# A Fourier layer tower on one core: three two-bank slots for the skip products, two banks for the transforms, and a new order of TensorE's work

## The reference

```python
v = concat([x, gx, gy]) @ p_w + p_b            # 3 features a pixel -> 32 channels
for i in range(4):
    x_ft = rfft2(v)
    out1 = einsum('bixy,ioxy->boxy', x_ft[:, :, :12, :12], W1)
    out2 = einsum('bixy,ioxy->boxy', x_ft[:, :, -12:, :12], W2)
    x1 = irfft2(out_ft)                        # out_ft: out1, out2, zero elsewhere
    x2 = einsum('bcxy,cd->bdxy', v, w_w[i]) + w_b[i]
    v = batch_norm(x1 + x2)
    if i < 3: v = relu(v)
h = einsum('bcxy,cu->bxyu', v, q_w) + q_b
```

## Time and profile before

| | us |
|---|---|
| median of 3 runs | 1845.2 |
| lowest and highest of them | 1844.68, 1857.29 |
| the profiled execution | 1830.84 |
| its span, first to last instruction | 1828.6 |
| PE, DVE, ACT, POOL busy | 1420.0, 686.7, 638.9, 289.6 |

### The profile page before, as it was taken

The page is one execution under the profiler, slowest core; times in us unless marked ns, Lnnn a source line. Parts: engine busy times, 40 slices in busy tenths (PEclk is TensorE's granted clock), DMA queues, the critical chain, the costliest instruction groups (busy, mean ns, idle before and its releaser), DMA issues.

```text
span 1828.6 us, 39520 instructions
## 1 busy us (share of the span) xinstructions
PE 1420.0 (78%) x18015; PEld 820.4 (45%) x18015; DVE 686.7 (38%) x678; ACT 638.9 (35%) x918; POOL 289.6 (16%) x405
## 2 busy tenths in 40 slices
PE   3567589999957779899875777888988488807887
PEld 3434266656533335555443333445545363207831
DVE  6432244554522224453442222444443231067443
ACT  1232145555522215555542221445545231000230
POOL 4630302021032200202204230020202231100000
PEclk8777699999977769999987776988989798955676
DMA  3668677777227869999943776999997316820001
GB/s 96 155 168 232 197 174 181 196 186 180 77 73 212 237 185 264 299 321 304 277 94 89 214 236 187 255 233 298 265 289 199 121 51 234 342 56 1 1 0 23
DMA packets 189377, 329.17 MB, mean 180 GB/s; under 512 B 27507, under 2 KB 133379, under 8 KB 170515
## 3 DMA queue, kind: packets, MB, share of 16 engines
q1 hardware_dynamic: 173644, 289.69, 57.4%
q0 software_dynamic: 15568, 36.98, 8.4%
HBM read 165.09 MB, written 142.64 MB: 168 GB/s over the span
## 4 chain that ended last, share of the span: by engine, by line
PE 60%; ACT 11%; DMA 11%; DVE 9%; issue 4%; SPq 3%; POOL 1%; DVEq 0%; ACTq 0%
PE ps L1332 10%; PE ps L1369 9%; PE ps L1294 6%; PE ps L1271 6%; DMA arena<-half_inverse 5%; PE ps L1389 5%; ACT ps L1172 4%; PE ps L1358 4%; PE ps L1280 3%; PE ps L1401 3%; ACT arena L1163 2%; PE ps L1447 2%; ACT arena L821 2%; PE ps L536 2%; DVE arena L821 2%
## 5 line engine op out<-in xcount | busy, mean ns | idle before, releaser
L1675 DVE STREAM_TRANSPOSE arena<-ps 128x1024 f32<-128x1024 f32 x96 | 179.1, 1950 | 422.7 <-PE ps L1389 422.7
L1036 POOL DMA_DIRECT2D arena<-arena x192 | 110.6, 584 | 891.8 <-ACT arena L1180 889.4
L1369 PE MATMUL ps<-arena 48*128 48x128 f32 x3072 | 212.2, 290 | 41.1 <-DMA arena<-half_inverse 30.2
L1369 PEld LDWEIGHTS ps<-arena 48*128 48x128 f32 x3072 | 191.9, 198 | 110.2 <-issue 69.9
L1163 ACT ACTIVATE arena<-ps,arena 128x1024 f32<-128x1024 f32 x128 | 147.4, 1202 | 262.5 <-PE ps L1369 256.9
L1172 ACT ACTIVATE ps<-ps 128x1024 f32<-128x1024 f32 x192 | 194.0, 1011 | 56.7 <-PE ps L1332 56.4
L1271 PE MATMUL ps<-arena 64*64 64x64 f32 x2304 | 144.8, 285 | 62.2 <-DMA arena<-arena 62.2
L1332 PE MATMUL ps<-arena 32*32 32x512 f32 x2944 | 187.9, 635 | 5.1 <-issue 4.6
L1271 PEld LDWEIGHTS ps<-arena 64*64 64x64 f32 x2304 | 136.3, 166 | 121.7 <-issue 121.7
L1665 DVE STREAM_TRANSPOSE arena<-arena 128x2048 f32<-128x2048 f32 x64 | 146.3, 2300 | 65.7 <-ACT arena L1163 41.0
L1389 PE MATMUL ps<-arena 32*32 32x512 f32 x3072 | 156.9, 606 | 5.7 <-DVE arena L1665 3.0
(11 more groups left out here) (286 smaller groups left out, 1317.7 us busy)
## 6 DMA issues: line engine op xcount, KB each, us to landing
maps<-arena SPq DMA_DIRECT2D x56, 1024.0 KB, 7.1
arena<-half_inverse SPq DMA_DIRECT2D x96, 384.0 KB, 11.1
half_inverse<-arena SPq DMA_DIRECT2D x33, 1024.0 KB, 6.1
maps<-inputs SPq DMA_DIRECT2D x28, 1024.0 KB, 11.6
arena<-maps SPq DMA_DIRECT2D x112, 256.0 KB, 9.0
inputs<-maps SPq DMA_DIRECT2D x112, 256.0 KB, 10.0
arena<-in_mode_w POOLq DMA_DIRECT2D x48, 384.0 KB, 3.9
arena<-maps SPq DMA_DIRECT2D x8, 2048.0 KB, 15.2
```

Of the source, the lines that this page charges most:

```text
L1369: last = nc.tensor.matmul(ps[:, b, at:at + 128], gtile[s][rows, 4 * b + 2 * h + n, :], iy[rows, :], start=False, stop=(i >= 2 and n == 1))
L1675: nc.vector.transpose(dst, src).then_inc(y_turned, 1)
```

## The change

1. Banks 0 to 3 in one set become three slots of two banks (0 and 1, 2 and 3, 4 and 5). A unit is now half of a half: `("out", q, h, p)` or `("next", q, h, p)`, where p names its rows of PE: 0 to 63 or 64 to 127. The eight units of a quad go round the three slots in the order of the table `UNITS`. A unit takes a slot once ACT is done with the unit three places earlier.
2. The y transform, the x transform and their results have only banks 6 and 7. The y transform is done in two parts e (rows 0 to 63, rows 64 to 127), and DVE must have turned part 0 before part 1 starts.
3. The inverse products of a unit (`inverse_part`) all read the same rows 64p to 64p+47 and are four in a row for each bank, so `turn_done` goes. For this the layouts of the modes and of `half_inverse` columns change (images b and b+32 in place of neighbours); the number and size of their DMAs stay.
4. The features of the first pass are fp32, 28 images and 3 grid rows in each group of 32 rows, in three blocks, loaded once near the start in 24 DMAs behind a memset of 128x3072 by POOL; no splitting by ACT and DVE. A skip product of the first pass is one fp32 product with 32 rows per bank.
5. The first pass stores a half of a map in four DMAs with rows of 2 KB, so that the second pass loads a half in one DMA with rows of 8 KB. The third pass loads as before. The two `group_load` calls near the end issue four DMAs each in place of two.
6. PE and ACT have a new order.

```diff
+        SLOTS_A = 3
+        def slot_of(l, kind, q, h, p):
+            n = PER_PASS * l + UNITS[kind, q, h, p]
+            return n % SLOTS_A, n // SLOTS_A + 1
...
-            def blocks32(w, source, h, pair, last_one):
+            def blocks32(w, source, h, p, s, last_one):
                 for x in range(4):
-                    for r in (2 * pair, 2 * pair + 1):
-                        rows = slice(32 * r, 32 * r + 32)
+                    for i in range(2):
+                        rows = slice(64 * p + 32 * i, 64 * p + 32 * i + 32)
...
-                            for g in range(4):
-                                at = 1024 * g + 512 * h
-                                nc.tensor.matmul(ps[:, g, :], w[:, 128 * (q % 8):128 * (q % 8) + 128],
-                                                 feats[q // 8][:, at:at + 512], start=(i == 0), stop=False)
+                    for i in range(2):
+                        rows = slice(64 * p + 32 * i, 64 * p + 32 * i + 32)
+                        nc.tensor.matmul(ps[:, 2 * s + i, :], expconv[rows, at:at + 128],
+                                         feats[QUAD * q // FEATURED][rows, 512 * h:512 * h + 512], start=True, stop=False)
...
+            def inverse_part(l, q, h, p, i):
+                s, n = slot_of(l, "out", q, h, p)
+                pe.wait_ge(g_in[q % 2], 32 * (slot_use(l, q) + 1))
+                rows = slice(64 * p, 64 * p + 4 * KY)
+                for k in range(4):
+                    last = nc.tensor.matmul(ps[:, 2 * s + i, 128 * k:128 * k + 128],
+                                            gtile[q % 2][rows, 8 * i + 4 * h + k, :], iy[rows, :], start=False,
+                                            stop=(k == 3))
+                if i:
+                    last.then_inc(a_full[s], 1)
...
+            def y_transform(l, q, e, yh):
+                if yh == 0:
+                    if e:
+                        pe.wait_ge(y_turned, 2 * n + 1)
+                    elif n:
+                        pe.wait_ge(xs_ev, 2 * n)
...
-                        for pair in range(2):
-                            sp.wait_ge(a_free[pair], set_of(l, "out", i, h) + 1)
-                        sp.dma_start(maps_d[l, ORDER[l][i], :, 2048 * h:2048 * h + 2048], half(h_out(l, i), h))\
-                          .then_inc(map_st[i % 2], 16)
+                        map_store(l, i, h)
                         if l:
                             input_load(l, i + 2, h)
```

More of the change, by code:

```diff
@@ L815, in staged, with per_map, stores, loads @@
             return (1 if batch % 2 == 0 else 0) + 2 * l + batch // 2
-        TURNS = (((0, 0), (1, 1)), ((0, 2), (1, 3)), ((0, 1), (1, 0)), ((0, 3), (1, 2)))
+        def per_map(l):
+            return 128 if l == 0 else 32
+        def stores(l, n):
+            return sum(MOVED * per_map(i) for i in range(l)) + n * per_map(l)
+        def loads(l, n):
+            return 16 * n if l == 1 else 16 * MOVED + 64 * n
         def inverse_evac(copy, ky, g):
-            return copy(xhalf[ky % 2].rearrange("p (g b h o) -> p g h b o", g=2, h=2, o=16)[:, g],
-                        ps[:, 6:8, :].rearrange("p h (o b) -> p h b o", o=16))
+            dst = xhalf[ky % 2].rearrange("p (q j s h o) -> p j h q s o", j=2, s=2, h=2, o=16)[:, g]
+            src = ps[:, 6:8, :].rearrange("p h (o q s) -> p h q s o", o=16, s=2)
+            return copy(dst, src)
+        BANKS = (0, 2, 1, 3)
         block = ctx.enter_context(nc.Block())
@@ L953, in _ @@
             for s in range(2):
-                sp.wait_ge(map_st[s], 32 * MOVED * PASSES)
-            for pair in range(2):
-                sp.wait_ge(a_full[pair], PER_PASS * PASSES)
+                sp.wait_ge(map_st[s], stores(PASSES, 0))
+            for s in range(SLOTS_A):
+                sp.wait_ge(a_full[s], slot_count(PASSES, s))
             stream_load(2)
@@ L1373, in next_set @@
-            def next_set(l, q, h):
-                for pair in range(2):
-                    free_pair(l, "next", q, h, pair)
-                    blocks32(wbd[l + 1], h_out(l, q), h, pair, True).then_inc(a_full[pair], 1)
-            def y_transform(l, q, yh):
+                        last = nc.tensor.matmul(ps[32 * x:32 * x + 32, 2 * s + i, :],
+                                                w[rows, 64 * p + 32 * i:64 * p + 32 * i + 32], source[rows, at:at + 512],
+                                                start=True, stop=last_one)
@@ new lines, in blocks32, with skip @@
+                return last
+            def skip(l, q, h, p):
+                s = take_slot(l, "out", q, h, p)
+                if l == 0:
+                    pe.wait_ge(conv_exp, 1)
+                    pe.wait_ge(f_in[QUAD * q // FEATURED], 16 * 8)
+                    for i in range(2):
+                        rows = slice(64 * p + 32 * i, 64 * p + 32 * i + 32)
+                        at = 128 * (q % (FEATURED // QUAD))
+                        nc.tensor.matmul(ps[:, 2 * s + i, :], expconv[rows, at:at + 128],
+                                         feats[QUAD * q // FEATURED][rows, 512 * h:512 * h + 512], start=True, stop=False)
+                elif q >= KEPT:
+                    pe.wait_ge(ld[q % 2][h], loads(l, q // 2))
+                    blocks32(wbd[l], h_in(l, q), h, p, s, False)
+                else:
+                    for i in range(2):
+                        at = 2048 * h + 512 * (2 * p + i)
+                        nc.tensor.matmul(ps[:, 2 * s + i, :], wbd[l], h_in(l, q)[:, at:at + 512], start=True, stop=False)
@@ L1502, in _ @@
             tt(exp3, exp3, prow.unsqueeze(1).broadcast_to([128, BATCH, CHANNELS]), ALU.add).then_inc(exp_ready, 1)
-            for row in (32, 96):
+            for row in range(FEATURED, 128, 32):
                 last = nc.vector.tensor_copy(prt[0:32, row:row + FEATURE_ROWS], pcol[0:32, 1:4])
@@ L1658, in turn_map @@
                 n = quad_of(l, q)
-                for pair in range(2):
-                    dve.wait_ge(a_free[pair], set_of(l, "out", q, h) + 1)
+                wait_free(dve, l, "out", q, h)
                 if n:
-                    dve.wait_ge(y_full, n)
+                    dve.wait_ge(y_full, 2 * n)
                 src = half(h_out(l, q), h).rearrange("p (b u y) -> p b u y", u=2, y=32)
@@ L1694, in _ @@
             dve.wait_ge(q_read, 2)
-            ts(placed[:, 60:64], image_of[:, 0:4], f1, None, ALU.mult).then_inc(z_ready, 1)
+            for j in range(2):
+                last = ts(placed[:, 30 + 32 * j:32 + 32 * j], image_of[:, 2 * j:2 * j + 2], f1, None, ALU.mult)
+            last.then_inc(z_ready, 1)
             dve.wait_ge(pm_ev, 2)
```

324 lines of the change are left out of this document (159 added, 165 removed).

## The result

The changed kernel takes 2145.3 us (median of four runs, 2123.3 to 2163.8) against 1844.9 us of the kernel before on the same chip: a ratio of 1.157, 95% interval 1.147 to 1.167. It is slower, as forecast, but by 300 us where 52 were forecast, and outside the range. (Now and then an execution of any of these kernels comes out one or two per cent longer at a lower granted clock; such runs are counted in the medians of this text but left out of its ratios, and every ratio is to the runs of the kernel before that were made beside it.) The profiled execution took 2152.4 us.

A forecast was written before the change was run, and what follows sets the result against it. PE was taken to bound the first pass, DMA engines or nearly the later two. Terms 37 + 2 + 12.5 + 3 - 3.5 + 1 = +52 on 1830.84 gave 1883 us (1897 as median), range 1868 to 1930.

The forecast's parts named there:

- The parts, first pass, one quad: PE's pieces in a first-pass quad, priced one by one: 19.45 us against 17.13, +37 us in 16 quads.
- three signs of being wrong: First-pass quad under 17 us, L1396 running beside L1420, or PE waiting for ACT L1204 or L1197 over 1 us a quad.
- the two terms named for it: Range terms: waits for the three slots, 0 to 1 us a quad, and the third pass, 0 to +12 us.
- the third pass at 0: Third pass, DMA engines full for 260 us: +3 us taken, 0 if all of PE's work is hidden.
- What the forecast took from the earlier trace: On PE, a change of shape lets the array run empty first, whichever rows are used; 0.84 us of wait seen.
- rival 1: On PE, shapes do not matter on disjoint rows, so units overlap: faster, -66 us, 1779 us; chance 0.15.
- Rival 2: On PE, the drain holds but units overlap better within a shape: first-pass quad 18.05, total 1860 us; chance 0.14.
- The y part's wait: y part 1 waits for DVE's turn of part 0: nothing mid-pass, about 1.9 us at a pass's end, +2 each pass.
- Rival 3: Two banks of y and x become the loop, next y waiting for ACT's copies: +48, 1945 us; chance 0.10.
- the term of -3.5: Feature casts go, one being on the chain with 3.49 us: -3.5 us, between -7 and 0.

The follow-up runs named there:

- rows64: Kernel after with 64 rows in place of 48 in each inverse product of the map passes, the added 16 times zero; 1951.0 us, 1.064 of before.
- probe2: Kernel before plus unread fp32 blocks holding the kernel after's quad pieces; in its order 491 us (clock 0.67), with 48x128 products in turn 269 us (1.00).
- feat: Kernel before with only the change's fp32 features in four groups of 32 rows; 1817.1 us, 0.976 of before.
- pair: Kernel after with both units' inverse products in turn on the two array halves and PE's pieces regrouped; 1798.1 us, 0.973 of before.
- pair64: The kernel pair with 64 rows in place of 48 in each inverse product, 16 of them times zero; 1785.5 us, 0.975 of before.
- probe: Kernel before plus unread fp32 product blocks of several shapes behind its last product; only 48x128 on one half ran at clock 0.50, for 123 us.
- probe3: Kernel before plus unread fp32 blocks varying rows and columns; one-half 48x128 ran at clock 0.50 (0.212 us per instruction), 64x128 at 1.00 (0.111).
- serial: Kernel before with all inverse products of one array half ahead of those of the other; 1944.9 us, one run.

## Why the prediction was wrong

**The step that failed** is the price list under "The parts, first pass, one quad". Every price there was read at a granted clock of 1.00 (in a pass at 0.98 by the earlier trace rows), and the sum took for granted that a PE with more to do and less to wait for would keep that clock. It did not: 0.71, 0.81 and 0.75 in the three passes. The forecast never named the clock of after as an unknown, so neither the range nor a rival held it, and of its three signs of being wrong (a quad under 17 us, L1396 beside L1420, waits for ACT) none came true. With the clock given back (rows64), 199 of the 322 us are gone. The lower end of the forecast's range, 1868, also lies below what the two terms named for it allow (the third pass at 0 gives 1894), which makes no difference here.

The Trainium skill, "TensorE: Matmul & The Clock Gate", section "What's actually happening", has the clock set "based on how busy the PE has been recently". The trace does not bear that out in the sense of the profile's busy share: 0.74 at 150.00 of 150 us busy here, 1.00 at 145.37 before.

**The rest, point by point.** rows64 shows what the change costs at full clock. One quad of its first pass:

```profile
404.73 1.07 PE ps L1380 x8
405.80 1.98 PE ps L1396 x16
407.78 1.06 PE ps L1380 x4
...
409.85 1.09 PE ps L1396 x8
410.94 1.02 PE ps L1420 x16
411.95 1.09 PE ps L1396 x8
...
414.10 2.53 PE ps L1396 x24
...
424.38 1.07 PE ps L1380 x8
```

- The quad: 19.65 us (424.38 - 404.73) against 19.45. The inverse is 1.98 + 1.09 + 1.09 + 2.53 + 1.09 = 7.8 against 7.7, the features 3.2 against 2.9. At full clock the sum of the price list was right to 1%, and its largest item, the inverse, too; the features were 0.3 too low.
- What the forecast took from the earlier trace rows held: the inverse at 411.95, on rows 0 to 63, starts only when the y part before it, on rows 64 to 127 (410.94), is through, and the 16 and 8 instructions cost what one half alone costs. So rival 1 is out.
- The second pass's best quads are 18.7 us in rows64 against 18.6. Rival 2, with 18.05 in the first, is out too.
- The sum, however, is not 1883: rows64's profiled execution is 1953.9. The first pass is 62 us longer than before, where 39 were forecast: its first two quads are at 0.50 until 284 us and take 27 and 33 us, some 21 more than two at full clock. Before, the clock rose at 237 us. The second pass is 35 longer (12.5 forecast) and the third 34 (3 forecast); there too the first two quads take long, 53 and 48 us together. That a new pass starts at 1.2 GHz, and that the new order leaves it later, is the same omission once more. Why 64 rows do not help in those two quads is open; no run was made for it. That they are entered at 0.50 may be part of it, since keeping the clock and bringing it up were not the same in probe2.
- The y part's wait costs nothing in the middle and comes back at the end of a pass, as forecast. In the chain of the kernel after, at the end of the first pass, DVE's turn L1712 stands twice, with y between:

```profile
646.91 1.91 DVE arena L1712
...
648.95 1.09 PE ps L1420 x16
...
651.26 1.90 DVE arena L1712
```

- Rival 3 did not happen: no wait of PE in the passes is put down to ACT's copies L1204, and ACT is no busier (638.5 us for 638.9).
- The feature cast of the earlier trace rows did not hold PE up, so the term of -3.5 was misread. The chain shows ACT's cast from 109.70 on, but PE's first inverse product along x started at 112.97, before that cast was through, and had waited for the transfer of the modes. Before:

```profile
112.97 2.08 PE L1294 MATMUL ps<-arena 48*128 48x512 f32 x4 [4.41 <-DMA arena<-mixed_modes]
```

and in the kernel after:

```profile
111.34 2.08 PE L1324 MATMUL ps<-arena 48*128 48x512 f32 x4 [5.07 <-DMA arena<-mixed_modes]
```

It starts 1.6 us earlier, released by the same transfer; the transfer had been issued 1.9 us earlier (103.64 for 105.56).
- The direction was right, and in part for the reason given: with the clock given back in the middle of the passes (rows64) the change still costs 123 us of span against the kernel before. The other 199 came from a cause that the forecast did not have. feat, pair and pair64 show that the change has good parts: the features are worth 1.4 us a quad, and the slots with the inverse in turn 1.0 more. What made it slower than before even in rows64 is its order, with one half of the array after the other (pair64, with the same rows in another order, takes 1785.5 us); what made it 16% slower is the clock that it lost besides.

## What to carry to other kernels

Before a price from a trace goes into a sum, write the granted clock beside it, and ask whether the change leaves the array as full as it was; if it doesn't, the sum needs a second column at 1.2 GHz. A PE that is busy in every slice of the profile can still run at half its clock, so read the PEclk row before the busy row. Where products must sit on one part of the array, put both parts in turn, keep products of one shape together, or add rows of zeros where the table has them: 16 inverse instructions take 1.98 us at 1.00 with 48 rows and with 64.

## What the runs showed of the hardware

- fp32 48x128 products on one half of the array ran at 0.50 for 123 us with PE busy throughout, and at 1.00 on both halves in turn. 64x128 products on one half ran at 1.00 (probe, probe3).
- 16 further rows, times zero, on the inverse products made a kernel 9% quicker (2145.3 to 1951.0 us).
- No product of another shape started before the block ahead of it was through, also where its rows were free: in rows64 8 inverse instructions on rows 0 to 63 and 16 y instructions on rows 64 to 127 follow each other at 1.09 and 1.02 us.
- 16 inverse instructions on one half and then 16 on the other took 3.43 us (serial, 0.107 each); in turn on both halves 1.99.
- 32x32 products on one half kept a clock of 1.00 (probe, probe3), and 14.6 us of them behind 48x128 products on one half did not bring it up from 0.50 (probe2).
